# An attention and FFN kernel whose 4-bit weights are decoded from 16-bit words, with the low halves made by VectorE, three units ahead

## The reference

```
low = W_packed & 15; high = W_packed >> 4 & 15
vals = NVFP4_LUT[idx].reshape(N, K // 32, 32) * scales[:, :, None]
gelu = 0.5*gate*(1 + tanh(0.79788*(gate + 0.044715*gate**3)))
out = (gelu * up) @ Wd.T
```

## Time and profile before

| | |
|---|---|
| median of 3 runs | 1632.79 us (1628.82 to 1633.92) |
| the profiled execution | 1631.91 us, its span 1630.0 us |
| TensorE busy | 1485.9 us, 91% |
| VectorE, ScalarE, GpSimd busy | 731.5, 762.5, 423.6 us |
| chain that ended last | PE 71%, DVE 9%, POOL 6% |

### The profile page before, as it was taken

How to read it: one execution, slowest core, us unless ns; L and a number is a source line. 1 busy time by engine, 2 the same in 40 slices (tenths; PEclk the granted TensorE clock), 3 DMA queues, 4 the chain that set the end, 5 groups by cost and what they waited for, 6 DMA issues and landing times.

```text
span 1630.0 us, 18890 instructions
## 1 busy us (share of the span) xinstructions
PE 1485.9 (91%) x7376; PEld 549.2 (34%) x7376; DVE 731.5 (45%) x870; ACT 762.5 (47%) x875; POOL 423.6 (26%) x274
## 2 busy tenths in 40 slices
PE   3788778899888888999999999999999999999998
PEld 1122222233323323333333333333333333444443
DVE  5777676867766663444333332433323311111111
ACT  1356565756664556555655455544444552111110
POOL 2012254745665574001111111011111111111111
PEclk8699899999999989999999999999999999999999
DMA  5122324433443243340223132343211110422310
GB/s 182 50 69 64 93 102 134 140 101 120 150 133 123 97 156 117 136 134 18 95 87 111 78 99 78 123 110 114 82 78 78 78 76 27 183 78 91 142 78 27
DMA packets 51130, 164.21 MB, mean 101 GB/s; under 512 B 7632, under 2 KB 16976, under 8 KB 50912
## 3 DMA queue, kind: packets, MB, share of 16 engines
q1 hardware_dynamic: 48192, 160.09, 28.9%
q10 hardware_dynamic: 2848, 2.90, 0.5%
HBM read 124.93 MB, written 37.77 MB: 100 GB/s over the span
## 4 chain that ended last, share of the span: by engine, by line
PE 71%; DVE 9%; POOL 6%; issue 4%; ACT 4%; DMA 3%; SPq 1%; ACTq 1%; POOLq 0%; DVEq 0%
PE psum L904 12%; PE psum L905 10%; PE psum L906 10%; PE psum L952 8%; PE psum L954 7%; PE psum L953 7%; PE psum L874 5%; POOL dq_w L395 4%; PE psum L844 4%; PE psum L860 4%; DVE dq_packed L428 2%; DMA wide<-seed_rows 2%; DVE dq_code L424 2%; PE psum L820 2%; ACT big L642 2%
## 5 line engine op out<-in xcount | busy, mean ns | idle before, releaser
L904 PE MATMUL psum<-y_hi,w_ring 128*128 128x512 f16 x1024 | 399.1, 390 | 40.6 <-POOL w_ring L414 23.7
L642 ACT ACTIVATE big<-psum 128x1024 f32<-128x1024 f32 x256 | 260.0, 1023 | 322.9 <-PE psum L860 311.1
L905 PE MATMUL psum<-y_lo,w_ring 128*128 128x512 f16 x1024 | 395.9, 387 | 0.0
L906 PE MATMUL psum<-y_hi,w_ring 128*128 128x512 f16 x1024 | 395.8, 387 | 0.0
L531 POOL TENSOR_TENSOR in_lo<-inter,in_hi 128x512 f16<-128x512 f32 x128 | 148.7, 1162 | 811.1 <-ACT in_hi L622 811.1
L711 DVE TENSOR_REDUCE maxima<-psum 128x2 f32<-128x1024 f32 x179 | 218.9, 1223 | 253.5 <-PE psum L844 253.5
L754 DVE SCALAR_TENSOR_TENSOR inter<-psum,gelu 128x512 f32<-128x512 f32 x128 | 88.2, 689 | 316.8 <-PE psum L906 300.9
L952 PE MATMUL psum<-w_ring,in_hi 128*128 128x512 f16 x512 | 196.9, 385 | 5.8 <-ACT gelu L615 3.1
L954 PE MATMUL psum<-w_ring,in_lo 128*128 128x512 f16 x512 | 195.9, 383 | 0.0
L953 PE MATMUL psum<-w_ring,in_hi 128*128 128x512 f16 x512 | 195.7, 382 | 0.0
L904 PEld LDWEIGHTS psum<-y_hi,w_ring 128*128 128x128 f16 x1024 | 100.4, 98 | 241.5 <-issue 114.8
(11 more groups left out here) (71 smaller groups left out, 1136.3 us busy)
## 6 DMA issues: line engine op xcount, KB each, us to landing
w_ring<-w_parts SPq DMA_DIRECT2D x96, 768.0 KB, 7.0
w_parts<-w_ring SPq DMA_DIRECT2D x32, 768.0 KB, 3.3
dq_packed<-packed SPq DMA_DIRECT2D x32, 384.0 KB
dq_scales<-scales SPq DMA_DIRECT2D x32, 384.0 KB
wide<-qk_parts SPq DMA_DIRECT2D x64, 128.0 KB
qk_parts<-wide SPq DMA_DIRECT2D x60, 128.0 KB
small<-x SPq DMA_DIRECT2D x8, 512.0 KB, 4.4
wide<-qk_parts SPq DMA_DIRECT2D x64, 64.0 KB
```

What stands on the lines that cost most here:

```text
L642: nc.scalar.activation(p_exp[:, k, :, i], p_score[:, bank:bank + 2, :], ACT.Exp, scale=SCORE_SCALE).then_inc(exp_done, 1)
L904: nc.tensor.matmul(dst, w[:, 0, k % 2, cols], hi, start=(k == 0), stop=False)
L905: nc.tensor.matmul(dst, w[:, 0, k % 2, cols], lo, start=False, stop=False)
L906: return nc.tensor.matmul(dst, w[:, 1, k % 2, cols], hi, start=False, stop=(k == TT - 1))
```

## The change

- The codes are given to the chip as 16-bit words: an int32 holds one byte of codes, and only its low 16 bits are kept. Two words lie in a uint32. A unit is 384 uint32 a partition in place of 768. VectorE masks the low nibbles' bits and signs (k = 0), then those of the high nibbles (k = 1), with four instructions that don't wait for one another, and joins signs and codes in one (k = 2). The values of the low nibbles and of the high nibbles now lie in two blocks, where they lay side by side.
- The scaling of the scales by ScalarE is left out; the constant goes into the high half and the low half.
- The low half is made by VectorE, with one scalar_tensor_tensor.
- AHEAD_UNITS is 3: unit 0 is decoded before the first maxima of batch 0, units 1 and 2 in batches 0 and 1. At unit u VectorE decodes unit u+3 in G0, G1 and G2, GpSimd multiplies in U0; the halves of unit u+2 are made in G1 (ScalarE) and G3 (VectorE). The loads, the stores and two places of PLAN move with it.

```diff
@@ -35,12 +35,12 @@
 IN_RING = GROUP + 1
-AHEAD_UNITS = 2
+AHEAD_UNITS = 3
 LAST_CHUNK = (CHUNKS - 1) * UNITS
...
 WORDS = 2 * P + 2 * P + 256
-DQ_STEPS = 4
+DQ_STEPS = 5
 STACK_DMAS = 10
@@ -63,9 +63,10 @@
         w_ring = sb("w_ring", [P, RING, 2, 2, WORDS], f16)
-        dq_packed = sb("dq_packed", [P, 2, WORDS], u32)
+        dq_packed = sb("dq_packed", [P, 2, WORDS // 2], u32)
         dq_scales = sb("dq_scales", [P, 2, WORDS], f32)
-        dq_code = sb("dq_code", [P, WORDS], u32)
+        dq_code = sb("dq_code", [P, 2, WORDS // 2], u32)
+        dq_sign = sb("dq_sign", [P, 2, WORDS // 2], u32)
         dq_w = sb("dq_w", [P, 2, WORDS], f32)
@@ -175,7 +176,6 @@
         dq_step = sem("dq_step")
-        scaled = sem("scaled")
         w_f_s = sem("w_f_s")
@@ -210,12 +210,12 @@
             "S30 m S31 m Q0a m Q0b m Q0h Q0l",
-            "X A2 m S00 m d0 K0a K0b m ws K0h S01 m S10 m A3 K0l AO m m S11 Y m MT MH ML S20 MV m S21 m Q1a YN m Q1b "
+            "X A2 m S00 m d0 K0a K0b m K0h S01 m S10 m A3 K0l AO m m S11 Y m MT MH ML S20 MV m S21 m Q1a YN m Q1b "
             "Q1h m S30 Q1l A0 m m A1 m S31 m",
-            "S00 d1 K1a m S01 m K1b K1h m S10 m F0 K1l S11 m A2 m d2 A3 MT AO m MH m S20 ML Y m S21 MV m V0a YN m "
+            "S00 K1a m S01 m K1b K1h m S10 m F0 K1l S11 m A2 m d1 A3 MT AO m MH m S20 ML Y m S21 MV m V0a YN m "
             "S30 m S31 A0 m m A1 m m",
-            "S00 m S01 d3 m A2 m m V0b S10 V0h m m A3 m AO S11 m MT m S20 m Y YN MH m ML U G1 S21 MV m S30 A0 m S31 m "
-            "A1 m m wh",
+            "S00 m S01 d2 m A2 m m V0b S10 V0h m m A3 m AO S11 m MT m S20 m Y YN MH m ML U G1 S21 MV m S30 A0 m S31 m "
+            "A1 m wh m wl",
         )
@@ -390,29 +390,24 @@
             pool.wait_ge(dq_step, DQ_STEPS * n + DQ_STEPS)
-            pool.wait_ge(scaled, n + 1)
             wait_from(pool, w_lo_s, n)
-            nc.gpsimd.tensor_tensor(dq_w[:, :, :], dq_code[:, :].bitcast(f16).rearrange("p (w e) -> p e w", e=2),
+            nc.gpsimd.tensor_tensor(dq_w[:, :, :], dq_code[:, :, :].bitcast(f16),
                                     dq_scales[:, n % 2].unsqueeze(1).broadcast_to([P, 2, WORDS]),
                                     ALU.mult).then_inc(w_f_s, 1)
-
-        def weight_scale(act, n):
-
-            act.wait_ge(dq_in[n % 2], 32 * (n // 2) + 32)
-            nc.scalar.activation(dq_scales[:, n % 2], dq_scales[:, n % 2], ACT.Copy,
-                                 scale=CODE_SCALE * W_SCALE).then_inc(scaled, 1)
...
                 act.wait_ge(w_out[n % RING], 16 * (n // RING))
-            wait_apart(act, act_spare, w_f_s, n + 1)
-            nc.scalar.copy(w_ring[:, n % RING, 0], dq_w[:, :, :]).then_inc(w_hi_s, 1)
-
-        def weight_lo(pool, n):
-            wait_apart(pool, pool_spare, w_hi_s, n + 1)
-            nc.gpsimd.tensor_tensor(w_ring[:, n % RING, 1], dq_w[:, :, :], w_ring[:, n % RING, 0],
-                                    ALU.subtract).then_inc(w_lo_s, 1)
+            act.wait_ge(w_f_s, n + 1)
+            nc.scalar.activation(w_ring[:, n % RING, 0], dq_w[:, :, :], ACT.Copy,
+                                 scale=CODE_SCALE * W_SCALE).then_inc(w_hi_s, 1)
+
+        def weight_lo(dve, n):
+            dve.wait_ge(w_hi_s, n + 1)
+            nc.vector.scalar_tensor_tensor(out=w_ring[:, n % RING, 1], in0=dq_w[:, :, :], scalar=CODE_SCALE * W_SCALE,
+                                           in1=w_ring[:, n % RING, 0], op0=ALU.mult,
+                                           op1=ALU.subtract).then_inc(w_lo_s, 1)
@@ -421,19 +416,14 @@
                 wait_from(dve, w_f_s, n)
-                nc.vector.scalar_tensor_tensor(out=dq_code[:, :], in0=raw, scalar=12, in1=raw,
-                                               op0=ALU.logical_shift_left, op1=ALU.bitwise_or).then_inc(dq_step, 1)
-            elif k == 1:
-                dve.wait_ge(dq_step, done + 1)
-                nc.vector.tensor_scalar(raw, dq_code[:, :], 12, 0x80008000, ALU.logical_shift_left,
+            if k < 2:
+                nc.vector.tensor_scalar(dq_code[:, k], raw, 9 - 4 * k, 0x0E000E00, ALU.logical_shift_left,
                                         ALU.bitwise_and).then_inc(dq_step, 1)
-            elif k == 2:
-                dve.wait_ge(dq_step, done + 2)
-                nc.vector.tensor_scalar(dq_code[:, :], dq_code[:, :], 9, 0x0E000E00, ALU.logical_shift_left,
+                nc.vector.tensor_scalar(dq_sign[:, k], raw, 12 - 4 * k, 0x80008000, ALU.logical_shift_left,
                                         ALU.bitwise_and).then_inc(dq_step, 1)
-            elif k == 3:
-                dve.wait_ge(dq_step, done + 3)
-                nc.vector.tensor_tensor(dq_code[:, :], raw, dq_code[:, :],
+            else:
+                dve.wait_ge(dq_step, done + 4)
+                nc.vector.tensor_tensor(dq_code[:, :, :], dq_sign[:, :, :], dq_code[:, :, :],
                                         ALU.bitwise_or).then_inc(dq_step, 1)
@@ -463,12 +453,11 @@
                             load_unit(sp, u + AHEAD_UNITS + 1)
-                        if UNITS <= u + AHEAD_UNITS + 1 < STEPS:
-                            reload_unit(sp, u + AHEAD_UNITS + 1)
+                        if UNITS <= u + GROUP - 1 < STEPS:
+                            reload_unit(sp, u + GROUP - 1)
                     elif step == "U2" and u + AHEAD_UNITS - 1 < UNITS:
-                        if u == 0:
-                            spill_unit(sp, 0)
-                        spill_unit(sp, u + AHEAD_UNITS - 1)
+                        for n in range(0 if u == 0 else u + AHEAD_UNITS - 1, u + AHEAD_UNITS):
+                            spill_unit(sp, n)
                     elif step == "U0" and c and u % UNITS == 1:
@@ -485,8 +474,8 @@
                     fill_stack(sp, b + 1, 1 - b % 2, 1, b > 0)
-                elif step == "U" and b == 0:
-                    load_unit(sp, 2)
+                elif step == "U" and b < SOLO:
+                    load_unit(sp, b + 2)
             store_rows(sp, CHUNKS - 1)
@@ -525,6 +514,7 @@
             x_low(0)
+            weight_f(pool, 0)
@@ -536,18 +526,14 @@
                         inter_low(u - 1)
-                    elif step == "G3" and SOLO <= u + AHEAD_UNITS - 1 < UNITS:
-                        weight_lo(pool, u + AHEAD_UNITS - 1)
-                    elif step == "U2" and u + AHEAD_UNITS < UNITS:
+                    elif step == "U0" and u + AHEAD_UNITS < UNITS:
                         weight_f(pool, u + AHEAD_UNITS)
...
                     x_low(b + 1)
-                elif step == "d3" and b < SOLO:
-                    weight_f(pool, b)
-                elif step == "wh" and b < SOLO:
-                    weight_lo(pool, b)
+                elif step == "d2" and b < SOLO:
+                    weight_f(pool, b + 1)
@@ -602,6 +588,7 @@
             store_qk(act, 0, 1, 1)
+            weight_hi(act, 0)
             max_part(0, 0, True)
@@ -626,9 +613,7 @@
                         inter_high(u - 1)
-                    elif step == "G1" and u + AHEAD_UNITS < UNITS:
-                        weight_scale(act, u + AHEAD_UNITS)
-                    elif step == "G2" and SOLO <= u + AHEAD_UNITS - 1 < UNITS:
+                    elif step == "G1" and SOLO < u + AHEAD_UNITS - 1 < UNITS:
                         weight_hi(act, u + AHEAD_UNITS - 1)
@@ -656,10 +641,8 @@
                     x_high(b + 1)
-                elif step == "ws" and b < SOLO:
-                    weight_scale(act, b)
                 elif step == "wh" and b < SOLO:
-                    weight_hi(act, b)
+                    weight_hi(act, b + 1)
@@ -741,7 +724,12 @@
             dve.wait_ge(dve_own, 10)
-            for n in range(16):
+            for k in range(3):
+                decode(dve, 0, k)
+            for n in range(8):
+                reduce_maximum(0, 0, n)
+            weight_lo(dve, 0)
+            for n in range(8, 16):
                 reduce_maximum(0, 0, n)
@@ -767,14 +755,10 @@
                     u, n = b, b + AHEAD_UNITS
-                    if step == "G1" and n < UNITS:
-                        decode(dve, n, 0)
-                    elif step == "G2" and n < UNITS:
-                        decode(dve, n, 1)
-                    elif step == "G3" and n < UNITS:
-                        decode(dve, n, 2)
-                    elif step == "U1" and n < UNITS:
-                        decode(dve, n, 3)
+                    if step[0] == "G" and step[1] in "012" and n < UNITS:
+                        decode(dve, n, int(step[1]))
+                    elif step == "G3" and SOLO < n - 1 < UNITS:
+                        weight_lo(dve, n - 1)
                     elif step == "U3":
@@ -794,7 +778,9 @@
                 elif step[0] == "d" and b < SOLO:
-                    decode(dve, b, int(step[1]))
+                    decode(dve, b + 1, int(step[1]))
+                elif step == "wl" and b < SOLO:
+                    weight_lo(dve, b + 1)
@@ -1034,7 +1020,7 @@
```

(3 more changed lines are left out.)

## The result

The changed kernel takes 1586.11 us (median of 4 runs, 1582.47 to 1589.26) against 1632.47 us: ratio 0.9719, 95% interval 0.9687 to 0.9750. The profiled execution took 1589.26 us, its span 1587.5; it was the slowest of the four. Forecast: 1579.

What follows compares the result with a forecast made beforehand. The prediction took the VectorE-GpSimd decoding loop to bound chunk 0. From 1631.9 us it took 58 for chunk 0 and added 2.5 for the start, 1576.4, and chose 1579 for late maxima; range 1563 to 1600.

Steps and rivals of the forecast that it cites:

- What bounds chunk 0, and how much there is to win: Chunk 0 of the FFN: weight decoding costs it 76.2 of 433.2 us, all that the change can win there.
- The loop, 11.4 us: Decoding in chunk 0: VectorE and GpSimd wait for and exclude each other, 11.4 us a unit against TensorE's 7.8.
- Masks 0.35, low half 1.74: VectorE's decoding: each 384-word mask takes 0.35 us, four 1.3, and the low half of 1536 elements 1.74.
- The multiplication u+3 is released by the OR: GpSimd's multiplication competes with VectorE's low half after the OR; low half first 70 to 30, loop 8.6 or about 10 us.
- Mean period 9.1: Time between GpSimd's multiplications in chunk 0, from weighing both orders 70 to 30: 9.1 us.
- Chunk 0 loses 18: Decoding still costs chunk 0 10 us from varying groups and 8 from late exponentials, maxima and clock; 58 won.
- The waits for low halves go, the high half is on time: Chunk 0: TensorE's 23.7 us of waits for low halves vanish; ScalarE's high half mostly just fits before VectorE needs it.
- Start +2.5: Before chunk 0: low half of unit 0 between maxima costs 1.7 us, decoding in batches 0 and 1 0.8.
- A: Rival: VectorE is no bound at all, chunk 0 runs as chunk 1, 3 us above; 1561 us, chance 0.18.
- B: Rival: GpSimd's multiplication goes ahead of the low half nearly every time, period 11.0; 13 us won, 1621, chance 0.16.
- C: Rival: VectorE's low half waits for ScalarE's late high half in most units, period 12.5; slower, 1669 us, chance 0.11.
- D: Rival: the loop shrinks but TensorE waits for something else in the same places; about 1631 us, chance 0.05.

Runs made afterwards that it cites:

- a_lopool: The changed kernel with the low half back on GpSimd at the same step, its scale left out: 1606.7 us, ratio 0.9852.
- b_words: The kernel before with the 16-bit words alone, low halves still on GpSimd and two units ahead: 1600.1 us, ratio 0.9837.
- a_nodecode: The changed kernel without decoding units 3 to 31, loads of codes and stores kept: 1556.2 us in one run, chunk 0 354.9 us.
- a_spread: The changed kernel with unit 0's low half before the first maxima and one unit of each four decoded inside the round of downs: 1575.7 us, ratio 0.9657.
- c_small_dqw2: The changed kernel with float16 scales and gelu, four slots for in_hi and in_lo, and two dq_w buffers: 1586.1 us, ratio 0.9714.
- b_lodve: The kernel before with the low halves made by VectorE instead of GpSimd, nothing else changed: 1610.8 us, ratio 0.9879.
- c_small: The changed kernel with float16 scales and gelu and four slots for in_hi and in_lo in place of five: 1584.5 us, ratio 0.9712.
- a_same: The changed kernel run again without any edit: 1585.2 us, ratio 0.9719.

## Why the prediction was right, and where it was off

- *What bounds chunk 0, and how much there is to win.* Right. The estimate of 357.0 us without decoding measured 354.9, the loss of 76.2 is 78.3.
- *The loop, 11.4 us.* Right. The two single edits that shorten the period shorten chunk 0, the one that leaves it leaves chunk 0 nearly as it was, and the one undone lengthens both (table). The mean period isn't the whole measure: a_lopool's is 0.4 below b_words', with the same chunk 0.
- *Masks 0.35, low half 1.74.* Right: 0.35 and 1.75, though four masks in a row take 1.15 and not 1.3. The exclusion by in_lo, put at 1.05, is 1.23 - 0.35 = 0.88 at 407.58. The multiplication, put at 3.44 as before, is 3.12: I didn't see that its input's stride goes away.
- *"The multiplication u+3 is released by the OR", 70 to 30 for the low half.* This step was wrong. The multiplication has a second wait, for the low half of the unit before, since dq_w is one buffer; the section on the kernel before says so, and the prediction didn't use it. So the low half can't meet it: the longest is 1.95 us, and none is in a second class at 3 to 5. The loop is masks, OR, low half, multiplication always in a row, the 8.6 us that I gave to 70 of 100; it measured 8.07. With two buffers the order is as I had argued: 21 multiplications held against five low halves.
- *Mean period 9.1.* It measured 9.07, and that is luck: the 30 of 100 long low halves that lift the forecast from 8.6 to 9.1 don't exist. The shortest periods are 8.05 to 8.08, the longest in a group 11.94; what lengthens each wasn't taken apart, and the last, 11.36, holds the wait for the load.
- *Chunk 0 loses 18.* It loses 24.2 (by the estimate of 357.0; 26.3 by a_nodecode), so 58 were forecast and 52.0 won. One term that was mis-sized is SP's queue, put at "nothing, bounds -1 and +2": the last four units lose 6.8 us against a_nodecode, with VectorE 6.9 us behind a load, and 0.9 in a_spread, where it doesn't wait. That is about the size of the whole miss, but it isn't isolated. The first 28 units lose 19.5 us, 2.8 a group, where 18/8 = 2.3 were forecast. Four periods are 4 x 9.07 - 31.2 = 5.1 behind TensorE, so a round of downs absorbs 2.3, not 4.9; the 1 us a group that I added for groups that vary, and the 8 us for late exponentials and maxima, made up for most of that. How it divides between these terms wasn't measured.
- *The waits for low halves go, the high half is on time.* Right: 23.7 to none on TensorE's matmuls (one of its weight loads still waits 0.8), 3.2 us of VectorE's waits for the high half in all.
- *Start +2.5.* It was +7.5, and 9.2 in a second execution, both the slowest of four. The part of it in the first maxima is real and near its forecast (1.5 us of 1.7). The rest wasn't found: with the low halves on GpSimd the start is 210.2, and moving two of them elsewhere gives 1 us.
- *Rivals.* A (no bound at all) falls: its condition came true, the low half never meets the multiplication, and still 26.3 us are left to the decoding, since the two stand in a row. B falls, since in the changed kernel the multiplication never goes ahead of the low half. C falls with the 3.2 us. D falls: loop and chunk 0 shrank together. The Trainium skill's rule of the shared port pair (SBUF — State Buffer, "Who interferes with whom") holds for a low half with two SBUF inputs: in c_small_dqw2 a multiplication that starts 0.16 us behind the low half takes 4.54 us in place of 3.09. It didn't speak against this change in the end, because the semaphore had put the two in a row before.

## What to carry to other kernels

Before you weigh two instructions against each other for a port, read every wait of both: a buffer that exists once may have settled their order already. When the steps of a loop wait for or shut out one another, its length is their sum (here 8.07 us), and moving the slower engine's share (3.2 us) to the faster one (1.75 us) pays even on an engine that is busier. A margin of one more unit gained nothing while the loop that fills it was longer than the consumer's; the place where nothing is decoded (here the round of downs) is the next thing to use. When work moves ahead, look where its loads now stand in the queue that issues them: one load behind ten others cost VectorE 6.9 us.

## What of the hardware was not expected

- GpSimd's multiplication of 128x1536 float16 by float32 takes 3.44 us when the float16 input has a stride of two (before, b_lodve), 3.12 when it lies in a row (changed, b_words), and 3.09 when both inputs are float16 (c_small).
- Kernels with one and the same program up to chunk 0 begin it at 219.2 and 220.9 us (changed, a_same), 213.9 (a_nodecode, which adds a GpSimd fill there), 216.4 and 222.9 (c_small, c_small_dqw2, whose start differs in float16 scales and the second buffer only). The kernels of the old kind lie at 205.8 to 211.7. The very first maximum begins at 38.26 us in the one and at 42.63 in the other of two executions of the same kernel. A difference of a few us in one profiled start shows nothing by itself; what makes these starts differ stays open.
